# Cross-attention and FP4 feed-forward on one core: the first softmax in two halves, five quads ahead of the stream instead of seven, block 1 two pieces longer

## What is computed

```python
f  = layernorm(x)
h  = tanh((ctx @ Ws)[:, None] + (f @ W)[:, :, None] + b)      # rows x 77 tokens x 512
rho = (h * w).sum(-1) + (1 - mask) * -1e30
txt = softmax(rho) @ ctx
x  = x + tanh(txt @ Wcw) * f + tanh(txt @ Wcb)
xn = layernorm(x)
g, u = fp4(xn) @ fp4(w_gate).T, fp4(xn) @ fp4(w_up).T         # 512 -> 1408
out = x + fp4(silu(g) * u) @ fp4(w_down).T                    # 1408 -> 512
```

## Time and profile before

| | us |
|---|---|
| median of 3 runs | 1537.94 (1537.92 to 1540.9) |
| the profiled execution | 1539.24 |
| its span, first to last instruction | 1537.4 |
| PE busy | 1432.1 (93%) |
| ACT busy | 1359.6 (88%) |
| DVE busy | 1157.2 (75%) |
| POOL busy | 248.7 (16%) |

### The profile page before, as it was taken

The page is one execution under the profiler, slowest core; times in us unless marked ns, Lnnn a source line. Parts: engine busy times, 40 slices in busy tenths (PEclk is TensorE's granted clock), DMA queues, the critical chain, the costliest instruction groups (busy, mean ns, idle before and its releaser), DMA issues.

```text
span 1537.4 us, 24122 instructions
## 1 busy us (share of the span) xinstructions
PE 1432.1 (93%) x9752; PEld 647.7 (42%) x9752; DVE 1157.2 (75%) x1783; ACT 1359.6 (88%) x1249; POOL 248.7 (16%) x389
## 2 busy tenths in 40 slices
PE   7988889856999999999999999989999999999998
PEld 4444444411333333334444444434444444555564
DVE  4699997944586666759666776698877787898887
ACT  5999989999999999999999999999999999433321
POOL 0122222200111010111011111011101111312211
PEclk9999999988999999999999999999999999999999
DMA  5133332320011111201111111112111111123332
GB/s 159 42 83 83 83 82 75 95 65 8 8 26 41 40 27 41 40 15 40 41 40 40 41 33 37 36 40 40 40 41 41 40 41 40 40 59 73 80 69 62
DMA packets 181557, 77.91 MB, mean 51 GB/s; under 512 B 163627, under 2 KB 165675, under 8 KB 181445
## 3 DMA queue, kind: packets, MB, share of 16 engines
q1 hardware_dynamic: 180224, 75.00, 21.0%
q10 hardware_dynamic: 1221, 1.36, 0.3%
HBM read 27.85 MB, written 8.39 MB: 24 GB/s over the span
## 4 chain that ended last, share of the span: by engine, by line
PE 52%; ACT 27%; DVE 17%; issue 2%; DMA 1%; POOL 1%; SPq 0%; ACTq 0%; DVEq 0%; POOLq 0%
PE rho L809 19%; ACT hring L628 17%; PE dn L906 10%; PE gu1g L892 5%; PE gu0g L892 5%; PE gu1u L892 5%; PE gu0u L892 5%; ACT hring L623 4%; DVE featT L985 2%; ACT wd_room L628 2%; DVE work L1019 2%; ACT featT L623 1%; ACT featT L628 1%; DVE work L1040 1%; DVE work L1039 1%
## 5 line engine op out<-in xcount | busy, mean ns | idle before, releaser
L628 ACT ACTIVATE hring<-featT,bias 128x1024 f32<-128x1024 f32 x688 | 729.2, 1156 | 2.6 <-PE rho L809 2.5
L809 PE MATMUL rho<-hring,wslide 128*32 128x512 f32 x3776 | 459.0, 611 | 61.5 <-ACT hring L628 52.4
L809 PEld LDWEIGHTS rho<-hring,wslide 128*32 128x32 f32 x3776 | 105.5, 111 | 338.6 <-issue 191.7
L628 ACT ACTIVATE featT<-featT,bias 128x1024 f32<-128x1024 f32 x220 | 236.3, 1178 | 2.2 <-PE rho L809 2.2
L906 PE MATMUL dn<-wd_room,turned 128*128 128x512 f16 x1023 | 230.6, 380 | 0.2 <-DMA turned<-work 0.2
L490 POOL TENSOR_SCALAR split_t<-sm 128x32 f32<-128x32 f32 (+4 forms) x82 | 19.7, 240 | 1178.1 <-DVE sm L1008 1178.1
L623 ACT ACTIVATE hring<-featT 128x4096 f32<-128x4096 f32 x57 | 207.5, 3640 | 0.4 <-DVE featT L985 0.4
L985 DVE TENSOR_SCALAR featT<-featT,bias 128x1024 f32<-128x1024 f32 x256 | 175.5, 750 | 11.9 <-ACT hring L623 7.6
L1309 DVE TENSOR_TENSOR work<-sg,gu1u 128x352 f32<-128x352 f32 x64 | 33.3, 521 | 173.9 <-ACT sg L661 173.1
L906 PEld LDWEIGHTS dn<-wd_room,turned 128*128 128x128 f16 x1023 | 96.4, 98 | 145.2 <-issue 36.0
L809 PE MATMUL rho<-featT,wslide 128*32 128x512 f32 x1056 | 126.4, 596 | 5.4 <-ACT featT L628 3.1
(11 more groups left out here) (228 smaller groups left out, 1578.5 us busy)
## 6 DMA issues: line engine op xcount, KB each, us to landing
xt<-in_x SPq DMA_DIRECT2D x32, 256.0 KB, 2.8
out<-xt SPq DMA_DIRECT2D x32, 256.0 KB, 2.3
work<-in_x SPq DMA_DIRECT2D x8, 512.0 KB, 4.1
xt<-in_x SPq DMA_DIRECT2D x6, 512.0 KB, 4.3
xt<-in_L_ffn_w_gate SPq DMA_DIRECT2D x11, 256.0 KB, 2.7
xt<-in_L_ffn_w_up SPq DMA_DIRECT2D x11, 256.0 KB, 3.0
work<-in_L_ffn_w_down SPq DMA_DIRECT2D x2, 704.0 KB, 5.1
xt<-in_L_ffn_w_down SPq DMA_DIRECT2D x2, 704.0 KB, 4.1
```

Source lines behind the costliest of these rows:

```text
L628: act.activation(slot[s][:, g, :], featT[:, e, ROW0[k]:ROW0[k] + rows], ACT.Tanh, bias=bias[:, e, base + tok:base + tok + 1]).then_inc(tan ...
L809: last = pe.matmul(rho[SLOTW * g:SLOTW * g + SLOTW, hf * 512:hf * 512 + 512], wslide[:, e, SLOTW - 1 - r:2 * SLOTW - 1 - r], slot[s][:, g, ...
```

## The change

It does four things. The softmax of block 0 goes in two halves of four tiles: sums, gates and factors of tiles 0 to 3, then DVE makes the first tile, then sums, gates and factors of tiles 4 to 7 follow; ACT gets two pairs of gates on four columns. Five quads are scored ahead of the stream, not seven. Block 1's scores end behind piece 4 of tile 6, not before piece 3 (`ENDS`), so block 2 begins two pieces later. And in tile 6, DVE's drain and shifts of block 1 move behind `hidden(6, 3)` into the quantisation of the hidden row, and the sums behind it; ACT issues the quads up to 156 before block 1's exponentials.

```diff
-PRE_QUADS = 7
+PRE_QUADS = 5
...
+    ENDS = [(0, -1), (BASE[1] - 2, 4), *((b - 2, 2) for b in BASE[2:])]
     for k in range(1, NBLK):
-        t0, p0 = (0, 0) if k == 1 else (BASE[k - 1] - 2, 3)
-        t1 = BASE[k] - 2
-        mine = [(t, p) for t in range(t0, t1 + 1) for p in range(7)
-                if (t, p) >= (t0, p0) and (t, p) <= (t1, 2) and not (t == 0 and p >= 4)]
+        mine = [(t, p) for t in range(NT) for p in range(7)
+                if ENDS[k - 1] < (t, p) <= ENDS[k] and not (t == 0 and p >= 4)]
...
+            def half_gates(hf, wanted, made):
+                act.wait_ge(wanted, 1)
+                part = slice(4 * hf, 4 * hf + 4)
+                for u in range(2):
+                    act.activation(gates[:, u, part], garg[:, u, part], ACT.Tanh, bias=bc[:, u:u + 1]).then_inc(made, 1)
+
             issued = EARLY
...
             softmax_exp(0)
             tanh_quad(issued, range(3, 4))
-            tanh_quad(issued + 1)
-            tanh_quad(issued + 2, range(0, 1))
-            softmax_gates(0)
-            tanh_quad(issued + 2, range(1, 4))
-            issued += 3
+            tanh_quad(issued + 1, range(0, 2))
+            half_gates(0, first_garg, first_gates)
+            tanh_quad(issued + 1, range(2, 4))
+            tanh_quad(issued + 2)
+            tanh_quad(issued + 3)
+            half_gates(1, garg_ready, gates_ready)
+            issued += 4
...
                 if t in SOFTMAX_AT:
-                    if issued < QUADS:
+                    goal = 2 * QPB + 3 if SOFTMAX_AT[t] == 1 else min(issued + 1, QUADS)
+                    while issued < goal:
                         tanh_quad(issued)
                         issued += 1
...
-                    if t in SOFTMAX_AT and p == 3 and t < FREE_FROM:
+                    ended = t in SOFTMAX_AT and t < FREE_FROM and p == ENDS[SOFTMAX_AT[t]][1] + 1
+                    if ended:
                         softmax_transposes(SOFTMAX_AT[t], 0)
                     for n in slots.get((t, p), ()):
                         score_quad(n)
-                    if t in SOFTMAX_AT and p == 3 and t < FREE_FROM:
+                    if ended:
                         softmax_transposes(SOFTMAX_AT[t], 1)
...
-            softmax_sums(0)
-            softmax_factors(0)
+            first_sums(0, first_garg)
+            first_factors(0, first_gates)
             rows_tile(0)
+            first_sums(1, garg_ready)
+            first_factors(1, gates_ready)
+            first_results(1)
...
-                    hidden(t, 1, sums=begun is None)
-                if begun is not None and t != FREE_FROM:
+                    hidden(t, 1, sums=begun is None or begun == 1)
+                if begun == 1:
+                    rows_tile(t + 1)
+                    hidden(t, 2)
+                    hidden(t, 3)
+
+                    def shifts():
+                        softmax_shift(1, 0)
+                        softmax_shift(1, 1)
+
+                    quantise_hidden(t, between=lambda: softmax_drain(1), midway=shifts)
+                    softmax_sums(1)
+                elif begun is not None and t != FREE_FROM:
                     softmax_drain(begun)
                     hidden(t, 2)
                     softmax_shift(begun, 0)
```

More of the change, by code:

```diff
@@ L307, in bass_xattn_fp4_ffn @@
         garg_ready = sem("garg_ready")
+        first_garg = sem("first_garg")
+        first_gates = sem("first_gates")
         gates_ready = sem("gates_ready")
@@ L1271, in softmax_factors, with first_sums, first_factors, first_results @@
                 step(tt(ga, ga, al, ALU.mult))
+            def first_sums(hf, made):
+                part = slice(4 * hf, 4 * hf + 4)
+                e = rhoS[:, hf * 512:hf * 512 + 512].rearrange("p (t s) -> p t s", t=4)[:, :, 0:TOK]
+                t = prod.rearrange("p (t s) -> p t s", t=4)[:, :, 0:TOK]
+                dve.wait_ge(exp_ready, hf + 1)
+                step(dve.tensor_reduce(den[:, part], e, axis=AX_X, op=ALU.add))
+                step(dve.reciprocal(den[:, part], den[:, part]))
+                for u in range(2):
+                    step(tt(t, e, uv[:, 0, u, :].unsqueeze(1).broadcast_to([P, 4, TOK]), ALU.mult))
+                    step(dve.tensor_reduce(garg[:, u, part], t, axis=AX_X, op=ALU.add))
+                    ins = tt(garg[:, u, part], garg[:, u, part], den[:, part], ALU.mult)
+                    if u == 1:
+                        signal(ins, made, 1)
+                    else:
+                        step(ins)
+            def first_factors(hf, made):
+                part = slice(4 * hf, 4 * hf + 4)
+                al, be, ga, va = (t[:, part] for t in (alpha, beta, gamma, var1))
+                var = stat[:, part, 1:2].rearrange("p t a -> p (t a)")
+                dve.wait_ge(made, 2)
+                step(tt(be, gates[:, 0, part], rstd[:, part], ALU.mult))
+                step(ts(al, be, 1.0, None, ALU.add))
+                step(tt(va, al, al, ALU.mult))
+                step(tt(va, va, var, ALU.mult))
+                rsqrt(ga, va, 4)
+                step(tt(ga, ga, al, ALU.mult))
+            def first_results(hf):
+                part = slice(4 * hf, 4 * hf + 4)
+                mean = stat[:, part, 0:1].rearrange("p t a -> p (t a)")
+                step(tt(beta[:, part], beta[:, part], mean, ALU.mult))
+                step(tt(beta[:, part], gates[:, 1, part], beta[:, part], ALU.subtract))
             def result_factors(k):
@@ L1300, in rows_tile @@
                 signal(quantise(hxn, D, xq[:, 0, :], xq[:, 1, :], hxn, SCALE_MIN, 1.0), xq_ready, t + 1)
-                if t in BASE[:-1]:
+                if t == 0:
+                    first_results(0)
+                elif t in BASE[:-1]:
                     result_factors(BASE.index(t))
```

## The result

The changed kernel takes 1547.45 us (median of 6 runs, 1546.35 to 1549.07), the kernel before 1538.54 us in the same session: ratio 1.0059, 95% interval 1.0048 to 1.0069. It is slower, as forecast, but by 8.9 us instead of 3.6, and outside the range. The profiled execution took 1548.61 us with a span of 1546.8, 9.4 over the span of before.

The account below looks back on a forecast made before the run. ACT was taken to bound the kernel until block 3's last quad, PE the rest. Stall 3.67 plus extra gates 0.38 minus block 1's 0.44 gave +3.6 us, 1541.6 us on the median's base; range 1538.3 to 1544.3 us.

Parts of the forecast that it names:

- The bound: Whole kernel: ACT sets the pace until block 3's last quad, busy 955.73 of 959 us; PE sets the rest.
- Start of the stream, ACT: Block 0's second gates: ACT stands 3.67 us waiting for DVE's garg; the extra pair of gates costs 0.38 us.
- the 4.05 us: Start of the stream: cost of splitting the gates on ACT, the stall and the extra pair together.
- -0.44 us: Block 1: ACT's wait for a DVE sum, taken as quad 92's, goes away, saving 0.44 us.
- I count nothing: Border of blocks 1 and 2: ACT does not wait at the exponentials and only 0.1 us at the gates, counted as zero.
- the forecast's 0.1 us: Border of blocks 1 and 2: gates wanted at E + 30.0, ready at E + 30.1, E being silu(6, 3)'s end.
- PE waits more at the transposes there and works it off in block 2: Border of blocks 1 and 2: PE's extra wait is recovered beside two pieces fewer in block 2; no cost was charged.
- Rival (c): Border of blocks 1 and 2: DVE 2 us late stalls ACT before exponentials or gates; 1543.5 us, chance 0.12.
- I keep them: Block 1: ACT's three waits for PE, 1.5 us, depend on how quads fall on pieces and were left unchanged.
- (a): Whole kernel: PE sets the end, so its earlier start makes the kernel faster, 1534.2 us; chance 0.11.
- (b): Before 1314 us: PE's lead removes all five ACT waits, returning 2.7 of 4.05 us; 1539.3 us, chance 0.13.
- (d): Start of the stream: no turned tile for PE at 374.5 us; sum unchanged up to 376.0; within the forecast's 0.64.

Follow-up runs that it names:

- e1: Changed kernel with ACT's second pair of gates four tanh later, behind quad 82's tanh; 1542.95 us, ratio 1.0026 to the kernel before.
- e2: Changed kernel with the sum of quad 101 allowed earlier, inside tile 1's quantisation on DVE; 1545.86 us, ratio 1.0045 to the kernel before.
- e4: Changed kernel with the edits of e1, e2 and e3 together; 1540.23 us, ratio 1.0007 to the kernel before.
- e9: Kernel before with DVE summing every third quad of block 2 instead of every fourth; 1541.38 us, ratio 1.0019.
- e10: Kernel before with denser DVE sums in block 3, 27 and two quads instead of 22 and two; 1537.82 us, ratio 0.9991.
- e5: Changed kernel with sums, gates and factors undivided again, five quads and later block end kept; 1547.63 us, ratio 1.0058 to the kernel before.
- e7: Kernel before with five quads ahead of the stream instead of seven; 1545.9 us, ratio 1.0043.
- e6: Changed kernel with block 1's old end and tile 6's old order, split gates and five quads kept; 1544.39 us, ratio 1.0044.
- e12: Changed kernel repeated word for word for a second profile; 1547.26 us in one run.
- e3: Changed kernel with both shifts of block 1's scores before quad 157's sum in tile 6; 1546.77 us, ratio 1.0050 to the kernel before.
- e11: The kernel of e4 with e9's denser sums in block 2; 1537.72 us, ratio 0.9999 to the kernel before.
- e8: Kernel before with only block 1's later end and tile 6's new order, undivided gates and seven quads; 1550.32 us, ratio 1.0075.
- e13: The kernel of e6 repeated word for word for a second profile; 1546.97 us in one run.

## Why the prediction was right and wrong

**The bound: right.** ACT's waits account for 8.9 of 9.1 us, the tail is unchanged, and taking waits away one by one gives each back (e1, e2, e4). This holds for work or waits added; work taken from ACT does not come back whole (e9, e10).

**Start of the stream, ACT: right, to the place and size.** Forecast 3.67 us before the second gates, measured 3.67; the first `gate_up` forecast at 374.5, measured 374.81; the first silu some 4 us sooner, measured 385.83 against 389.81. The extra gates cost 0.39 from start to start, for a forecast of 0.38.

**What the prediction read out of that was wrong, though the sum was not touched by it.** It called PE's earlier start worth nothing and charged the 4.05 us to the split. e5 and e7 show that the two quads taken from the head are the cost: they were ACT's cover while the first tile is made. The split, by starting PE sooner, avoids 4.91 us of waits, 2.56 of them made by the lower clock in e5, and costs 4.38; with its second pair four tanh later it costs next to nothing (e1: 1542.95 us against 1547.63 in e5). The split with seven quads was not run. The Trainium skill (Perfetto Trace Analysis, Optimizing Scalar/DVE Operations) says that breaking up instructions can let work complete sooner where Scalar or Vector aren't saturated but cause bubbles on other engines; the prediction put this place under its other half, grouping on a saturated engine. By e1 and e5 the first half was the one to use: between the gates and the first silu DVE's chain, and the transfer and `gate_up` behind it, set the end, not ACT.

**Block 1, "-0.44 us": wrong, the first failed step.** It came out as +2.24, 2.68 off. In the kernel before the wait is this:

```profile
440.92 3.62 ACT L623 ACTIVATE hring<-featT 128x4096 f32<-128x4096 f32 x1 [0.44 <-DVE featT L985]
```

It was not for quad 92 but for 98, the fourth summed quad that ACT takes in block 1. That it would go came true, by luck, since another quad had been followed. And only this one wait was followed through the new order. The next quad, 101, was left out: the plan's count moved from 99 to 96 and its sum fell out of the quantisation (e2 puts it back, e6 does so by the old end).

**Border of blocks 1 and 2, "I count nothing": wrong, the second failed step.** It came out as +2.30 in the profiled execution and 1.15 in e12 (0.31 + 0.61 + 0.49 - 0.26). The prediction followed DVE's time to the exponentials and the gates; neither waits there. For the gates that is partly because ACT itself came late: without the wait at the ring they wait 0.75 us in e3 and e4, whose order on DVE differs a little, so the forecast's 0.1 us is not confirmed. It did not follow PE: the transposes wait 3.19 us for the shift behind a sum, the matmuls behind that idle run slow (4.04 us instead of 2.11), and the ring of buffers carries this to ACT; the 0.31 and 0.50 us beside it are there in every profile of the late end but e3, e4 and e11, which have the 0.31 alone. The sentence "PE waits more at the transposes there and works it off in block 2" is the step that failed: ACT had by then written all three buffers of block 2's ring and could go no further. Rival (c) named the place and about the price (2 us), but DVE as the cause, and its sign, an idle before exponentials or gates, did not come: the idle stands before a tanh.

**"I keep them", the three waits for PE:** five now, with 0.72 us more, the 0.22 and the 0.50 of the ledger.

**Rivals (a) and (b)** fall: nothing came back. (d) did not occur. The range missed because each of the two steps added 2.3 us; without them it would be 1547.45 - 2.24 - 2.30 = 1542.9 us, inside it.

## What to carry to other kernels

Where one engine is busy 99.7% of a stretch, list everything that it waits for under the new order, through every summed tile and every buffer that it reuses, not only the waits that the old trace shows: here the two that were not listed cost more than the one that was. Work that stands ahead of a first use is cover; before it is cut, work out when the chain beside it is done. And a change of an integer plan is judged row by row: its parts don't add, and undoing some of them can bring nothing (e5) or be worse than keeping all (e8). A difference that comes from one profile is set against a second profile of the same kernel before it is believed.

## What was not expected of the hardware

After an idle of PE the next matmuls can take nearly twice their time: 12 of 352 columns took 3.52 us after 3.89 us and 3.68 after 2.87, 1.95 otherwise. In the stretch table of the changed kernel the granted clock from 685 to 690 us is 0.50, the lower of the two levels (1.2 GHz):

```profile
685.00:690.00 5.00, 4.45 (x15) 2.80 (x16) 2.71 (x4) 4.98 (x6) 0.00 (x0) 0.50 0.00 0
```

What was new is that the same order and the same idle give more of it in one execution than in another (4.04 and 3.60 us in the changed kernel), or all of it in one kernel and none in another (4.44 us in e6, 2.75 in e7), and that through a ring of buffers this reaches another engine: 0.61 to 2.23 us of ACT's time. The Trainium skill (TensorE: Matmul & The Clock Gate, What's actually happening) says that the monitor behind the clock runs free of the kernel, so that a transition falls differently from run to run; e12 against the first profile agrees, and e13, which repeats e6 within 0.03 us, does not speak for it.
